# A decoder layer on one core: maxima in one block, values and denominators in one stationary block, residual in the free rows

## The reference, cut

```python
def attn(x):                                   # H = 16, DK = 8
    # Q, K: linear, 3-tap conv, projection; V: linear
    tau   = sigmoid(conv(gelu(conv3(x)), tau2))    # per query and head
    delta = sigmoid(conv(gelu(conv3(x)), del2))    # per key and head
    scores = einsum('bhqd,bhkd->bhqk', Q, K) / sqrt(DK)
    scores = scores * tau[..., None] + delta[:, :, None, :]
    out = einsum('bhqk,bhkd->bhqd', softmax(scores), V)
    return linear(out.transpose(0, 2, 1, 3).reshape(b, l, D), out_w, out_b)
x = layernorm(x + attn(x))
x = layernorm(x + xattn(x, ctx, ctx))          # gates, cumulated log-forget, running maximum
x = layernorm(x + mx_quantize(x) @ mx_quantize(W).T + bias)
```

## Time and profile before

| | us |
|---|---|
| median of 3 runs | 238.55 (237.43 to 240.87) |
| profiled execution | 238.0 |
| its span, first to last instruction | 236.3 |
| TensorE busy, share | 208.4, 88% |
| VectorE / ScalarE / GpSimd busy | 154.1 / 134.2 / 132.0 |
| mean granted TensorE clock | 0.949 of full |
| `res` on POOL, one (L347) | 0.97 |
| store of a result, issue to landing | 1.9 |

### The profile page before, as it was taken

One profiled execution on the slowest core, in us unless ns is written; L12 is line 12 of the kernel. 1 busy time (PEld: TensorE's weight loads), 2 busy tenths in 40 slices (PEclk: granted clock), 3 DMA queues, 4 the chain that ended last, 5 costly groups with the idle time before them and its releaser, 6 DMA issues. The chain is left out here.

```text
span 236.3 us, 5909 instructions
## 1 busy us (share of the span) xinstructions
PE 208.4 (88%) x2217; PEld 132.0 (56%) x2217; DVE 154.1 (65%) x354; ACT 134.2 (57%) x346; POOL 132.0 (56%) x239
## 2 busy tenths in 40 slices
PE   1799889699999999899888899789889969699895
PEld 1676454244566455566546567366648756276552
DVE  4587889959444553557647779966684475556871
ACT  2632867556854643673763768757776465515332
POOL 7994629691232192581695848862781757523520
PEclk9997999979999999999999999999997967899799
DMA  5822110000000000202002003003002003000001
GB/s 145 206 37 78 47 47 0 1 0 3 0 3 3 0 3 1 92 3 81 11 1 94 3 1 115 0 25 97 23 0 67 28 8 103 3 22 1 22 1 47
DMA packets 10220, 8.40 MB, mean 36 GB/s; under 512 B 1872, under 2 KB 9264, under 8 KB 10192
## 3 DMA queue, kind: packets, MB, share of 16 engines
q1 hardware_dynamic: 8816, 7.83, 11.2%
q0 software_dynamic: 512, 0.18, 0.7%
q10 hardware_dynamic: 864, 0.01, 0.2%
HBM read 6.94 MB, written 1.08 MB: 34 GB/s over the span
## 5 line engine op out<-in xcount | busy, mean ns | idle before, releaser
L996 DVE TENSOR_REDUCE nm<-score 128x8 f32<-128x1024 f32 x32 | 39.1, 1223 | 22.0 <-PE score L740 22.0
L511 ACT ACTIVATE prob<-score 128x1024 f32<-128x1024 f32 x32 | 32.6, 1021 | 21.2 <-PE score L755 21.0
L740 PE MATMUL score<-km,qf 32*128 32x512 f32 x128 | 35.0, 640 | 0.8 <-ACT prob L511 0.7
L750 PE MATMUL score<-qm,kf 32*128 32x512 f32 x128 | 35.0, 639 | 0.8 <-DVE nm L996 0.8
L775 PE MATMUL pvb<-ones 128*128 128x512 bf16 x80 | 23.5, 436 | 0.0
L359 POOL CAST nmx<-nm 128x16 bf16<-128x16 f32 x16 | 4.1, 254 | 30.4 <-DVE nm L996 30.4
L381 POOL TENSOR_TENSOR u<-u,maskb 128x1024 f32<-128x1024 f32 x7 | 16.5, 2358 | 7.2 <-DMA u<-gates_out 7.2
L768 PE MATMUL pvb<-prob,vz 128*32 128x128 f32 x512 | 17.4, 277 | 2.2 <-ACT prob L511 2.2
L859 PEld LDWEIGHTS qkb<-ctm,cc 128*128 128x128 f32 x128 | 15.3, 194 | 4.3 <-issue 2.2
L768 PE MATMUL pvb<-prob,ez 128*32 128x128 f32 x512 | 16.9, 273 | 0.0
L859 PE MATMUL qkb<-ctm,cc 128*128 128x33 f32 x128 | 15.7, 278 | 1.3 <-DVE cc L1069 0.8
(11 more groups left out here) (248 smaller groups left out, 485.8 us busy)
## 6 DMA issues: line engine op xcount, KB each, us to landing
u<-gates_out SPq DMA_DIRECT2D x7, 512.0 KB, 3.7
xt<-in_x_dram SPq DMA_DIRECT2D x4, 256.0 KB, 4.3
cin<-in_ctx_dram SPq DMA_DIRECT2D x4, 256.0 KB, 3.4
out_dram<-th SPq DMA_DIRECT2D x8, 128.0 KB, 1.9
ck<-in_L_attn_convk_w_dram SPq DMA_DIRECT2D x1, 192.0 KB, 3.6
cq<-in_L_attn_convq_w_dram SPq DMA_DIRECT2D x1, 192.0 KB, 3.9
pk<-in_L_attn_kproj_w_dram SPq DMA_DIRECT2D x1, 128.0 KB, 2.9
pq<-in_L_attn_qproj_w_dram SPq DMA_DIRECT2D x1, 128.0 KB, 3.4
```

The costliest lines, as they stand in the source:

```text
L511: nc.scalar.activation(prob[:, n % 2, 2 * h:2 * h + 2, :].rearrange("p g s -> p (g s)"), sc[:, 1024 * h:1024 * (h + 1)], ACT.Exp, scale=0. ...
L740: ins = mm(sc[:, 512 * q:512 * (q + 1)], qf[r, n, :], km[r, n % (2 * CB)].rearrange("p j s -> p (j s)"), start=True, stop=True)
L750: mm(sc[:, 512 * q:512 * (q + 1)], kf[r, m, :], qm[r, m % (2 * CB)].rearrange("p j s -> p (j s)"), start=True, stop=False)
L996: nc.vector.tensor_reduce(nm[:, n % RING, 8 * h:8 * (h + 1)], sc[:, 1024 * h:1024 * (h + 1)].rearrange("p (h s) -> p h s", h=8), AX_X, ALU ...
```

## The change

The computation stays the same. What changes:

- **Maxima in one block.** `split` writes its three parts side by side into one block of 128 columns; one transpose replaces four, the ACT copy is of 128 columns instead of 512, and the broadcast is done for each head group j by a selecting stationary block `sel[r, j]`: 8 matmuls of 128 columns a half instead of 2 of 512.
- **One stationary block for a head's values and denominators.** `ve` holds 16 columns a head, 8 for values and 8 for exp(delta), so one pass of 16 matmuls in `pv` gives both, in interleaved rows of `pvb`. DVE's `stream_shuffle` (stage `dn`) brings the denominators beside the numerators; Ln and Exp on ACT and `att` now run over 128x512 instead of 128x256. Exp's bias `dcol` makes the result zero in the rows of the denominators.
- **Residual in the free rows.** These rows of `att` take the residual: `xs` holds `xTr` in them, put there by 64 DMAs from SP (16 a chunk), and POOL (stage `xa`; DVE's `xal` for the last pair) adds it. `xTr` has two chunk buffers instead of four. `y1` is four matmuls as before, with a weight `wcC` made at the start.
- **At the start** there are more small copies, four products of 128x128 and four of 8 columns on PE; POOL clears `xs` (4096 columns) instead of `ez` (2560).
- **Filler.** A `warm` turn has one matmul instead of two, and there are 87 in the order instead of 80.
- `PLACES` is another table throughout.

The diff, cut; `PLACES` shows in the order below.

```diff
-    "ph": (22, 23, 33, 36, 42, 45, 48, 52, 56, 59, ...
+    "ph": (19, 20, 23, 31, 41, 44, 47, 51, 54, 57, ...
...
@@ block.sync
+                if (c := due("xs", t)) is not None:
+                    sp.wait_ge(resid, c + 1)
+                    if c == 0:
+                        sp.wait_ge(vzero, 1)
+                    for r in range(2):
+                        for i in range(DK):
+                            sp.dma_start(xs[DK + i::VB, CB * c:CB * (c + 1), r, :], xTr[64 * r + i:64 * (r + 1):DK, c % 2]).then_inc(xs_in[c], 16)
@@ block.gpsimd
+                    if c >= 2:
+                        pool.wait_ge(xs_in[c - 2], 32 * DK)
+                    nc.gpsimd.tensor_scalar(xTr[:, c % 2], xTp[:, CB * c:CB * (c + 1), 1:S + 1],
...
+                if (p := due("xa", t)) is not None:
+                    pool.wait_ge(att_done, p + 1)
+                    pool.wait_ge(xs_in[p // 2], 32 * DK)
+                    nc.gpsimd.tensor_tensor(att[:], att[:], xs[:, 2 * p:2 * p + 2], ALU.add).then_inc(xa_done, 1)
@@ block.scalar
-                    nc.scalar.activation(nmT[:, n % RING, :], trb[:, 0:J * S // 2].bitcast(BF16), ACT.Copy).then_inc(nmT_sb, 1)
+                    nc.scalar.activation(nmT[:, n % RING, :], trb[:, 0:S // 2].bitcast(BF16), ACT.Copy).then_inc(nmT_sb, 1)
...
-                    link(nc.scalar.activation(ld[:], pvb[:].rearrange("p (v t s) -> p v t s", v=2, t=2)[:, :, 1, :], ACT.Ln))
-                    nc.scalar.activation(rec[:], ld[:], ACT.Exp, scale=-1.0).then_inc(rec_done, 1)
+                    act.wait_ge(dn_done, p + 1)
+                    link(nc.scalar.activation(dn[:], dn[:], ACT.Ln))
+                    nc.scalar.activation(dn[:], dn[:], ACT.Exp, bias=dcol[:, 0:1], scale=-1.0).then_inc(rec_done, 1)
@@ block.tensor
-                        for q in (2 - 2 * h, 3 - 2 * h):
-                            r = slice(32 * q, 32 * (q + 1))
-                            ins = mm(sc[:, 512 * q:512 * (q + 1)], ones[r, :], nmT[r, m % RING, :], start=False, stop=True)
+                        for j in range(J):
+                            for q in (2 - 2 * h, 3 - 2 * h):
+                                r = slice(32 * q, 32 * (q + 1))
+                                ins = mm(sc[:, 512 * q + S * j:512 * q + S * (j + 1)], sel[r, j, :], nmT[r, m % RING, :], start=False, stop=(j == J - 1))
...
-                    for k, w in enumerate((vz, ez)):
-                        o = 2 * S * (n % 2) + S * k
-                        for j in range(J):
+                    for r in range(2):
+                        o = 2 * S * (n % 2) + S * r
+                        for i in range(2):
                             for q in range(G):
-                                ins = mm(pvb[32 * q:32 * (q + 1), o:o + S], w[:, G * (n % 4) + q, 32 * j:32 * (j + 1)],
-                                         prob[:, n % 2, q, S * j:S * (j + 1)], start=(j == 0), stop=(j == J - 1))
+                                ins = mm(pvb[32 * q:32 * (q + 1), o:o + S], ve[:, G * (n % 4) + q, 64 * r + 32 * i:64 * r + 32 * (i + 1)],
+                                         prob[:, n % 2, q, S * (2 * r + i):S * (2 * r + i + 1)], start=(i == 0), stop=(i == 1))
...
-                    pe.wait_ge(att_done, p + 1)
-                    pe.wait_ge(resid, p // 2 + 1)
+                    pe.wait_ge(xa_done, p + 1)
...
-                        mm(yb[:, (D + 2 * NH) * v:(D + 2 * NH) * (v + 1)], att[:, v, :], woC[:], start=True, stop=False)
-                        ins = mm(yb[:, (D + 2 * NH) * v:(D + 2 * NH) * (v + 1)], xTr[:, 2 * p + v, :], cent[:], start=False, stop=True)
+                        for r in range(2):
+                            ins = mm(yb[:, (D + 2 * NH) * v:(D + 2 * NH) * (v + 1)], att[:, v, r, :], wcC[:, r, :], start=(r == 0), stop=(r == 1))
@@ block.vector
+                if (p := due("dn", t)) is not None:
+                    dve.wait_ge(pv_done, 2 * p + 2)
+                    if p > 0:
+                        dve.wait_ge(att_done, p)
+                    nc.vector.stream_shuffle(dn[:], pvb[:], [VB * (k // VB) + DK + k % DK for k in range(32)]).then_inc(dn_done, 1)
...
-                    nc.vector.tensor_tensor(att[:], pvb[:].rearrange("p (v t s) -> p v t s", v=2, t=2)[:, :, 0, :], rec[:],
-                                            ALU.mult).then_inc(att_done, 1)
+                    nc.vector.tensor_tensor(att[:].rearrange("p v r s -> p (v r s)"), pvb[:], dn[:], ALU.mult).then_inc(att_done, 1)
+                if (i := due("xal", t)) is not None:
+                    p = LATE + i
+                    dve.wait_ge(att_done, p + 1)
+                    dve.wait_ge(xs_in[p // 2], 32 * DK)
+                    nc.vector.tensor_tensor(att[:], att[:], xs[:, 2 * p:2 * p + 2], ALU.add).then_inc(xa_done, 1)
```

More of the change, by code:

```diff
@@ L32 @@
 PAIRS = B // 2
-VS = 40
+VB = 2 * DK
 CW = DH + 1
@@ new lines @@
+    "exps": (51, 53, 56, 58, 61, 64, 67, 71, 76, 77, 82, 85, 88, 93, 96, 102, 104, 106, 114, 118, 122, 125, 131, 138, 140, 142, 146, 150, 158, 163, 168, 169),
[6 rows of a table added]
+    "mkk": (0, 3, 4, 5, 10, 11, 12, 13, 29, 31, 35, 36, 51, 54, 56, 57), "res": (1, 2, 14, 16),
+    "mkq": (6, 7, 8, 9, 17, 18, 19, 20, 40, 41, 42, 43, 61, 62, 63, 64),
+    "split": (15, 21, 27, 32, 39, 46, 48, 52, 60, 67, 73, 77, 83, 87, 94, 97),
[4 rows of a table added]
+    "xs": (0, 1, 2, 3), "spread": (4, 5, 6, 7, 10, 11, 13), "store": (8, 9, 12, 14, 15, 16, 17, 18),
@@ L252, in _ @@
                 load_c(c)
-            for t in turns("spread", "store"):
+            for t in turns("xs", "spread", "store"):
+                if (c := due("xs", t)) is not None:
[5 more added lines that the diff above has]
+                            sp.dma_start(xs[DK + i::VB, CB * c:CB * (c + 1), r, :], xTr[64 * r + i:64 * (r + 1):DK, c % 2]).then_inc(xs_in[c], 16)
                 if (p := due("spread", t)) is not None:
@@ L324, in _ @@
             pool.wait_ge(init_sb, 1)
-            for t in turns("mkk", "mkq", "res", "ez", "gcb", "split", "dma", "dm", "z2", "x2", "x2b", "xd", "out"):
+            for t in turns("mkk", "mkq", "res", "ez", "xa", "gcb", "split", "dma", "dm", "z2", "x2", "x2b", "xd", "out"):
                 if (i := due("mkk", t)) is not None:
@@ L773, in _ @@
                     pe.wait_ge(*pved)
-                    for k in range(2):
-                        mm(pvb[:], ones[:], ones[:].unsqueeze(1).to_broadcast([P, 512 // P, P]), start=True, stop=True)
+                    mm(pvb[:], ones[:], ones[:].unsqueeze(1).to_broadcast([P, 512 // P, P]), start=True, stop=True)
                 if (n := due("nmT", t)) is not None:
```

120 lines of the change are left out of this document (68 added, 52 removed), and 47 rows, old and new, of the table PLACES.

## The result

The changed kernel takes 260.6 us at the median against 238.0 for the kernel before in the same runs: a ratio of 1.094, 95% interval 1.085 to 1.104. It is 9% slower, where 227.0 and a range of 218 to 238 were predicted. The profiled execution takes 259.6 us, with a span of 257.8 (before: 236.3). All ratios here are of the faster executions of each kernel, since single executions of one kernel differ by up to 4%, so a ratio can differ a little from that of the medians beside it.

A forecast was written before the change was run, and what follows sets the result against it. It took PE to bound the loop; first piece -8.2, middle -1.4, last -4.1, start +1.6, chain +1.5 and tail -0.5 gave -11.1 us, from 238.0 to 226.9, stated as 227.0, range 218 to 238.

The forecast's parts named there:

- The loop is PE's: Loop over 16 batches: PE is busy for 109.7 of 118.6 us and bounds it, with 8.9 us of idling.
- -15.1 us of PE work: Loop's `pv`: 16 matmuls do values and denominators instead of 32, 0.94 us for 1.89 a batch, 15.1 us saved.
- +1.5 us for the chain: Loop: the chain from `pv` to `y1` gets 2.7 us longer, mostly without loss; 1.5 us charged.
- 2.7 kept back in the middle: Middle piece of the loop: with DVE at 88% it shrinks by 1.4 us, not the 4.1 PE would give back.
- DVE and POOL take the bound over: Rival, chance 0.19: DVE cannot pass 80% in the loop's middle, waiting on POOL's additions; 233.0 us, range 231 to 237.
- PE stands in the hand-overs: Rival, chance 0.07: each pair's next `pv` or `y1` waits for the longer chain in full; 247 us.
- the rival of the loads: Rival, chance 0.07: the maxima's broadcast is bound by its stationary loads, 0.81 us a half; 239.7 us.
- +1.6: Start: four more PE products of 128x128 and four of 8 columns add 1.6 us.
- the transfers: Start: 64 residual DMAs on the sync queue hold POOL until 51.3 us but cost nothing, with 5.5 us of cover.
- -0.5: Tail: pair 6 starts earlier, the last `att` chain is longer; -0.5 us net, bounds +3 and -7.
- tail forward: Rival, chance 0.10: pair 6 comes early by its 4 us and the loop has no stall; 219 us or less.
- -11.1 us on record: Whole kernel: the sum of all terms for loop pieces, start, chain and tail, from 238.0 to 226.9 us.

The follow-up runs named there:

- f4: The kernel before with each VectorE maximum taken over half the keys: 235.6 us against 238.0.
- e2: The kernel before with the value product of a batch cut from four accumulated quarters to one: 240.3 us, before 238.5.
- i1: Changed kernel with POOL's additions cut in four, PE fillers in nine places, and POOL's third and fourth residual steps moved later: 234.8 us, ratio 0.995.
- e4: The kernel before with its old content put in the changed kernel's order: 255.4 us beside 238.5 for the kernel before.
- e3: The changed kernel's operations in the order of the kernel before, shuffle and residual steps placed: 256.3 us beside 238.5 for the kernel before.
- h2: The kernel before in the changed kernel's order, with POOL's additions cut in four and the same fillers as g4: 245.3 us, ratio 1.023.
- g4: The changed kernel with POOL's mask and gate additions cut in four and PE fillers in nine places: 235.4 us, ratio 0.990 to the kernel before.
- e1: The changed kernel with every value and denominator product issued twice, some 15 us more PE work: 266.0 us.
- h3: g4 with fillers in four more places: 236.9 us, ratio 1.003.

## Why the prediction was wrong, step by step

**"The loop is PE's."** Right, with a condition that was not seen. f4 took 17 us of maxima from VectorE and got 1.9; e2 took 11.3 from PE and got most of it, wherever the clock stayed full. The condition is the clock: the prediction valued each PE step at prices of the full clock and took it that the clock would stay. **This is the step that failed.** It read the rows of PEclk in the earlier trace rows as a state of before and not as something that the change acts on. Its largest term, -15.1 us of PE work, was to come off in full; the lower clock costs an estimated 24 us in the loop, more than the loop's whole growth of 22.6. The second term that failed is the one for waits, +1.5 us for the chain and 2.7 kept back in the middle: PE idles for 13.7 us more, and in the loop it waits 6.3 us for `prob`, 3.8 for `lf`, 3.3 for `cc` and 2.5 for `nG`. A low clock stretches PE's work and a gap brings the low clock on, so the two cannot be told apart to the microsecond.

**The order.** The prediction had the key in the earlier trace rows, 2.04 us beside an addition for 0.17, and used it only for how full VectorE can get in the middle and for its first rival. It did not go through the new order and ask which VectorE operations now stand beside POOL's additions, and who waits behind them. These were `lf`, `gb` and the fp8 product. As groups by line, changed kernel (busy us, mean ns):

```profile
L911 DVE TENSOR_TENSOR x<-x,qs 128x256 fp8e4<-128x256 f32 x8 | 7.1, 890 | 0.3
...
L1121 DVE TENSOR_SCALAR hn<-hn 128x8 f32<-128x8 f32 x8 | 5.7, 713 | 0.3
...
L1060 DVE TENSOR_TENSOR gb<-x,gcb 128x16 f32<-128x16 f32 x8 | 5.3, 663 | 1.2 <-ACT x L546 1.2
```

Before they took 434, 203 and 316 ns on average. (Of `hn` little is new: its next operation takes 373 ns for the 722 that it took before. `lf` has 355 for 344; what is new there is that PE waits for it.) The rival "DVE and POOL take the bound over" pointed at the right pair of engines, at 233.0; its mechanism, a full VectorE, was not it, for VectorE is busy for 91.1 of 141.2 us. The rival "PE stands in the hand-overs", 247, had the right sign and the wrong place: PE waits for `lf` and `cc`, for `att` hardly (1.6 us in all).

**The prices** were mostly right:

```profile
L778 PE MATMUL score<-nmT,sel 32*128 32x128 bf16 x256 | 15.1, 246 | 0.0
...
L392 POOL TENSOR_TENSOR att<-att,xs 128x512 f32<-128x512 f32 x7 | 8.8, 1264 | 4.1 <-DVE att L1049 4.1
...
L1044 DVE STREAM_SHUFFLE dn<-pvb 128x512 f32<-128x512 f32 x8 | 5.8, 724 | 0.0
L531 ACT ACTIVATE dn<-dn,dcol 128x512 f32<-128x512 f32 x8 | 5.8, 722 | 0.3
```

The shuffle is 0.72 us for 0.69, `xa` 1.26 for 1.1, Exp 0.72 and Ln 0.63 for 0.59, `att` 0.67 for 0.69. One `pv` group takes 1.01 us for the 0.94 worked out, so 14.1 us come off there for the 15.1. The eight broadcast products of a half take 0.32 us at the full clock (53.15 to 53.47), the lower bound, where 0.41 was taken. So the rival of the loads falls. The rule that it leaned on, "TensorE: Matmul & The Clock Gate" of the Trainium skill, section "LDWEIGHTS (loading the stationary operand)", gives the time of one load, and the trace agrees with it: a load of such a block is shown at 0.10 us. What failed is the prediction's step from there to eight loads unhidden, one behind the other, 0.86 us.

**The start.** "+1.6" became +4.4. Not the transfers: POOL stood until 51.15, where 51.3 was worked out (by two misses that cancel: the issues begin at 29.44 and not 35.5, and take 0.63 us each and not 0.43), and this cost nothing (i1). The new order sets the third and fourth `pk` product ahead of the loop. Each takes 2.8 us (from 79.24 to 82.02 in the trace of before), 5.6 us that the loop no longer has, so the loop's own loss is so much larger than its 22.6 us show. e4, which has no such transfers, starts its first `pv` at 74.48; e3, which has the added copies and products in the old order, at 68.42, so the +1.6 us taken for these products is not seen at all. The places of `pk` were in the table and were overlooked.

```profile
51.15 1.52 POOL L358 TENSOR_SCALAR xTr<-xTp,rcol 128x512 f32<-128x512 f32 x1 [7.59 <-DMA xs<-xTr]
```

**The tail.** -0.5 was taken; it is -5.5, at nearly the same clock (0.88 for 0.86): the rival "tail forward", at -6.5, had this right. The fillers there are 80 in both kernels, 40 turns of two and 80 of one, not 87 against 80. No run takes the tail's gain apart.

**The content** was judged rightly: -11.1 us on record, -9.9 as measured between h2 and g4 where the clock holds (in the loop -8.9 for -12.2, the rest in start and tail). The prediction laid it on a kernel in which it could not be had. That the total agrees to about a microsecond is in part luck, since the loop, the start and the tail each came out otherwise.

## What to carry to other kernels

Where PE bounds a stage with waits of under a microsecond between its products, as here, taking work off it is worth its price only as long as the granted clock stays up: look in the trace for where the new gaps will be, and at what stood ahead of the falls that are there already. A long POOL instruction beside small VectorE operations on SBUF is worth cutting into pieces before anything else (16 us here, with the same work); go through a new order for the pairs that it sets side by side and for who waits behind them. A filler helps only in the gap and only in a bank whose last reader is done; elsewhere work costs time (e1) or makes a new gap (h3).
